# A histogram and a scatter moved between stages of a graph network kernel

## The chip, the cores and the metric

The kernel runs on one core of a Trainium2 chip. The metric is the time of one execution on the device in microseconds (us), the median of several runs. The core has five engines with an instruction stream each: PE (TensorE, matrix products), DVE (VectorE, elementwise), ACT (ScalarE), POOL (GpSimd, which here mostly issues indirect DMAs) and SP (SyncE, which issues plain DMAs and counts). They meet only in semaphores and in a barrier at the end of each block of code. `then_inc(s, n)` adds n to a semaphore when an instruction is done, a DMA adds 16 when it has landed, and `wait_ge(s, n)` holds an engine's stream.

## The reference

```
h0 = layernorm(x)                                     # x: 12500 nodes x 256
x1 = x + segment_sum(h0[src] * edge_weight, dst) @ W.T + b      # 200000 edges, dst sorted
y  = layernorm(x1)
h  = (y @ W_gat).reshape(M, 4 heads, 4 experts)
a_src, a_dst = (h * att_src).sum(-1), (h * att_dst).sum(-1)
e  = leaky_relu(a_src[src2] + a_dst[dst2], 0.2)       # 131072 unsorted edges + a loop per node
alpha = softmax of e over the edges of each destination
agg = segment_sum(h[src2] * alpha, dst2) + b_gat
scores = layernorm(agg).mean over heads;  the 2 best of 4 experts get softmax weights g
out = x1 + sum over experts of g * (gelu(y @ W1 + b1) @ W2 + b2)
```

## The kernel before

12,500 nodes are 98 tiles of 128. Six blocks of code run one after the other, with a barrier of all engines between them.

`layernorm_and_plan` normalises x into `feats` and computes which steps the next block takes. `weighted_sums` goes through the 200,000 sorted edges in 391 groups of 4x128. For each group POOL issues four indirect gathers of 128 rows of `feats` (L511) into a ring of 8 groups (`RING`); `refill(g)` waits until PE has done the last step of group g-8 (`s_mm`). SP waits for each group's gathers to land and then adds to `s_ready`, for which PE waits. For each of 488 steps (a group and a node tile) DVE builds four weighted one-hot matrices (`one_hots`, L685 and L689) at most 4 steps ahead of PE (`XS`), and PE multiplies them with the rows (L645). Where a tile ends, PE closes it and runs `stages` (L617 to L637), and ACT reads the results (`tile`), in the end h without its scale in `node_row`. Between stretches of steps DVE also sorts the 131072 second-layer edges by destination: `sort_piece(n)`, n = 0 to 23, one after each of 24 stretches, where a piece with `columns(.., 10)` is 20 TENSOR_TENSORs in a row. From piece 9 on PE turns the keys in between (L664); PE waits for the whole piece before that (`s_turn`). The whole block is 33 such stretches, of which the last 9 are one loop.

`attention_terms` scales h by 1/std, forms the attention terms of sources (`node_row`, last 4 columns) and of destinations (`node_dst`), stores both (L824), and fills `adst_first` with zeros (8 DMAs from ACT, L838).

`gather_and_experts`: POOL gathers the source's 20 values for all 131072 sorted edges, 1024 indirect DMAs (L1120), which SP moves into `states` (L1093). Meanwhile PE, ACT and DVE run the four experts of 39 of the 49 pairs of tiles (`pair`). In the first 32 pairs DVE also builds 0/1 matrices of the edges' destinations (`hots`, L1285: 16 TENSOR_TENSORs for 32 columns of edges, each with two inputs in SBUF), and PE adds up their products (`count`, L1247) to a histogram: how many edges each node has. `positions` turns it into the first and last place of each node's edges in the sorted list. After its gathers, POOL scatters the destinations' terms to those first places in `adst_first`: 98 indirect DMAs (L1139) in 14 sets of 7, each set after two small copies.

`segment_softmax` begins with the load of `adst_first` and of the last value from `adst_dram`; its scans run on DVE, with 4 pairs of experts beside them. `combine` gathers the nodes' results, weighs the experts and writes the output.

Of the kernel before, what the change touches and what calls it, by code (L numbers as in the profile page):

```python
# [5 lines left out]
F32 = mybir.dt.float32  # L6
# [32 lines left out]
HCOLS = 32  # L39
# [9 lines left out]
EARLY_PAIRS = 39  # L49
SCAN_PAIRS = 4  # L50
# [26 lines left out]
def build(nc, x, src, dst, edge_weight, W, b, W_gat, att_src, att_dst, b_gat, gamma, beta,  # L77
# [14 lines left out]
    with ExitStack() as top:  # L92
# [28 lines left out]
        with ExitStack() as part1:  # L121
# [12 lines left out]
            weighted_sums(nc, sem, feats, edge_index, x, W, b, W_gat, W1, b1, W2, b2, m)  # L134
            attention_terms(nc, sem, att_src, att_dst, m)
# [258 lines left out]
def weighted_sums(nc, sem, feats, edge_index, x, W, b, W_gat, W1, b1, W2, b2, m):  # L394
# [11 lines left out]
    with ExitStack() as ctx:  # L406
# [27 lines left out]
        squares = sb("squares", [P, FEAT])  # L434
        psA = pb("node_sums", 1024)
        psT = pb("turned", GCOLS)
        psS, psX, psY, psH = pb("sums_turned"), pb("x1_product"), pb("xc_turned"), pb("h_product")
# [10 lines left out]
        s_w, s_wt, s_wte = sem("b_weights"), sem("b_w_turned"), sem("b_w_ready")  # L448
        s_tile = sem("b_tile_summed")
# [8 lines left out]
        PIECES = 24  # L458

        CUT = [1 + (QUADS - 1) * n // (PIECES + 9) for n in range(PIECES + 1)] + [QUADS]  # L460
# [17 lines left out]

        @block.sync
        def _(sp):  # L480
# [4 lines left out]
            sp.dma_start(brow[:], b.rearrange("(a n) -> a n", a=1)).then_inc(s_w, 16)  # L485
            for k in range(HALVES):
                sp.dma_start(m.w1[:, k, :, :], W1[:, k * P:(k + 1) * P, :].rearrange("e p n -> p e n")
                             ).then_inc(s_experts, 16)
# [8 lines left out]

            with sp.Fori(1, full_rounds + 1) as i:
# [6 lines left out]
            sp.wait_ge(s_experts, 16 * (HALVES + FB + 2 * EXPERTS))  # L505

        @block.gpsimd
        def _(pool):
# [12 lines left out]
            for g in range(RING):  # L521
# [5 lines left out]
                            allow_small_or_imprecise_dtypes=True))  # L527
            pool.wait_ge(s_pc, c.n)

            for t in (sums, sums_t, xc, xc_t, xs[:, 2:XS, :]):  # L530
                c.inc(pool.memset(t[:], 0.0))
            c.inc(pool.affine_select(out=shift_dn[:], in_=shift_dn[:], compare_op=ALU.not_equal, fill=1.0,
                                     base=1, pattern=[[-1, P]], channel_multiplier=1))
            for g in range(RING, GROUPS):
                refill(g)

        @block.scalar
        def _(act):
# [47 lines left out]
            act.wait_ge(s_w, 16 * 3)  # L586
# [8 lines left out]
            with act.Fori(1, LOOPED) as u:  # L595
                for r in range(XS):
                    tile(u * XS + r, r)
            for j in range(LOOPED * XS, TILES + 4):
                tile(j, j % XS)
            for par in range(2):  # L600
# [3 lines left out]
        def _(pe):  # L604

            pe.wait_ge(s_w, 16 * 3)
# [6 lines left out]
            pe.wait_ge(s_pc, 9)  # L613
# [39 lines left out]

            open_or_close(0, True)
            for r in range(XS):
                step(r, r)
            for n in range(PIECES):
                with pe.Fori(CUT[n], CUT[n + 1]) as u:
                    for r in range(XS):
                        step(u * XS + r, r)  # L660
                if n >= 9 and n < PIECES - 1:
# [5 lines left out]

            pe.wait_ge(s_turn, PIECES - 9)
            pe.matmul(psT[:, 0:2], shift_dn[:], lastd[:], start=True, stop=True).then_inc(s_turned, 1)
            with pe.Fori(CUT[PIECES], CUT[PIECES + 1]) as u:  # L670
                for r in range(XS):
                    step(u * XS + r, r)
# [5 lines left out]
        def _(v):  # L678
# [14 lines left out]
            def sort_init():  # L693
                v.wait_ge(s_ei, 32)
                c.done(v.tensor_scalar(key_i[0], key_i[0], KEY_SHIFT, KEY_TOP, ALU.logical_shift_left,
# [3 lines left out]
                v.wait_ge(s_pc, 9)  # L699
# [87 lines left out]

            for r in range(XS):
# [3 lines left out]
            for n in range(PIECES):  # L792
# [3 lines left out]
                buf = sort_piece(n, buf)  # L796
            sort_end(buf)
            with v.Fori(CUT[PIECES], CUT[PIECES + 1]) as u:
                for r in range(XS):
                    one_hots(u * XS + r, r)  # L800

def attention_terms(nc, sem, att_src, att_dst, m):

    with ExitStack() as ctx:
        def sb(name, shape, dt=F32):
# [979 lines left out]
```

## Time and profile before

| | |
|---|---|
| runs shown (3) | 4170.54, 4172.11, 4172.34 us; median 4172.11 |
| the profiled execution | 4173.15 us, of which the profile's span is 4171.6 |
| busy in the span | PE 3043.3 us (73%), DVE 1862.1 (45%), ACT 711.1 (17%), POOL 2771.7 (66%) |
| mean PE clock | 0.859 of full speed |

A POOL instruction that issues an indirect DMA is shown as busy for some 0.95 us, with 0.30 us ahead of it that the profile calls "issue"; such a row stands for 1.25 us of POOL's time. Names in a row are the program's tiles, `out<-in`. A "q" behind an engine's name is its instruction queue. Each value of PE, both weights and data, is 32 bits wide in the steps, and the profile shows one product as two MATMUL records, so one step of four products is "x8". The ends of MATMULs are modelled, and some records can be missing.

### The profile page before, as it was taken

To read this page: it belongs to the slowest core of one execution; us is meant where nothing else is said; L and a number is where in the kernel's file an instruction comes from. 1 tells how busy PE (TensorE), PEld (TensorE's weight loads), DVE (VectorE), ACT (ScalarE), POOL (GpSimd) and SP (SyncE) were. 2 spreads that over 40 slices of the span, in tenths; PEclk is the share of its full clock that TensorE was granted. 3 is DMA by queue.
4 is the path that set the end of the run, shared out by engine and by line. 5 is a ranking of instruction groups with operands and counts; after the bars stand their busy time and mean duration, and the time that the engine had idled before them with its cause. 6 is when DMAs were issued, how large, how long until landed. Compare 5 with 4: busy or idle time off the path is not lost. (4 is left out here: it accounts for less than half of the span.)

```text
span 4171.6 us, 58590 instructions
## 1 busy us (share of the span) xinstructions
PE 3043.3 (73%) x13541; PEld 2403.4 (58%) x13542; DVE 1862.1 (45%) x4572; ACT 711.1 (17%) x1985; POOL 2771.7 (66%) x2844
## 2 busy tenths in 40 slices
PE   1356666777788887889869999999999700175946
PEld 0234444555566665666658888888888600154734
DVE  6233344535555556434434444444431000387749
ACT  4000000000111111222222222222222100031412
POOL 0677777777777777777747777777777777300850
PEclk6677878888978998999989999999999855587968
DMA  7533333344444444444422222222222210003839
GB/s 252 163 104 106 108 109 111 114 114 114 116 116 119 121 121 120 127 127 127 130 87 63 60 63 60 65 63 60 63 61 66 48 19 5 31 23 154 311 139 358
DMA packets 298251, 450.16 MB, mean 108 GB/s; under 512 B 61256, under 2 KB 232339, under 8 KB 297491
## 3 DMA queue, kind: packets, MB, share of 16 engines
q0 software_dynamic: 114144, 216.61, 21.1%
q1 hardware_dynamic: 83238, 137.78, 9.2%
q10 hardware_dynamic: 100749, 94.40, 6.9%
q8 instruction: 48, 0.79, 0.1%
q14 instruction: 72, 0.59, 0.0%
HBM read 330.48 MB, written 105.96 MB: 105 GB/s over the span
## 5 line engine op out<-in xcount | busy, mean ns | idle before, releaser
L511 POOL DMA_INDIRECT rows<-feats,src_t x1564 | 1506.1, 963 | 589.6 <-issue 464.5
L645 PE MATMUL node_sums<-rows,hot 128*128 x3904 | 1088.3, 435 | 452.2 <-SPq L501 428.2
L645 PEld LDWEIGHTS node_sums<-rows,hot 128*128 128x128 f32 x3904 | 809.2, 215 | 694.1 <-issue 567.6
L1120 POOL DMA_INDIRECT got<-row_dram,src_sorted x1024 | 994.6, 971 | 311.9 <-issue 311.9
L689 DVE TENSOR_SCALAR hot<-iota,rel,ew_t 128x128 f32<-128x128 f32 x1952 | 558.5, 363 | 64.7 <-DVE rel L685 1.8
L1210 PE MATMUL d_hidden<-d_yt,w 128*128 128x256 f32 x2496 | 569.0, 382 | 0.8 <-DVE d_yt L1310 0.8
L1221 PE MATMUL d_expert<-w,hid 128*128 128x256 f32 x2496 | 564.1, 379 | 0.0
L685 DVE TENSOR_SCALAR rel<-dst_t,step_base 128x4 f32 x488 | 126.8, 260 | 976.5 <-PE node_sums L645 924.3
L1221 PEld LDWEIGHTS d_expert<-w,hid 128*128 128x128 f32 x2496 | 475.1, 190 | 63.6
L1210 PEld LDWEIGHTS d_hidden<-d_yt,w 128*128 128x128 f32 x2496 | 471.3, 191 | 62.0 <-DVE d_yt L1310 1.2
L1295 DVE TENSOR_TENSOR yo<-d_expert,b2r 128x512 f32<-128x512 f32 x156 | 107.9, 692 | 705.2 <-PE d_expert L1221 705.2
L1164 ACT ACTIVATE hid<-d_hidden,b1c 128x256 f32<-128x256 f32 x624 | 262.0, 471 | 887.2 <-PE d_hidden L1210 887.2
L553 ACT COPY sums<-node_sums 128x256 f32<-128x256 f32 x98 | 36.5, 372 | 1691.1 <-PE sums_turned L637 1691.1
L960 PE MATMUL scan_ps_y_turned<-ident,scan_y 128*128 128x128 f32 x16 | 2.9, 313 | 310.3 <-ACT scan_y L897 310.3
L960 PEld LDWEIGHTS scan_ps_y_turned<-ident,scan_y 128*128 128x128 f32 x16 | 2.2, 160 | 311.0 <-ACT scan_y L897 310.7
L1622 POOL DMA_INDIRECT ns<-state_dram,last_pos x98 | 155.7, 1589 | 30.4 <-issue 29.6
L1285 DVE TENSOR_TENSOR hot_lo<-iota_b,lo 128x512 bf16<-128x512 bf16 x256 | 160.7, 697 | 0.0
L1618 POOL MEMSET ns<- 128x2352 f32 x1 | 2.1, 2057 | 237.3 <-POOLq L1362 237.3
L1743 DVE SCALAR_TENSOR_TENSOR xs<-ys,sc,xs 128x256 f32<-128x256 f32 x392 | 156.2, 479 | 5.5 <-DMA xs<-x_dram 4.9
L1455 DVE COPY decay<-adfirst 128x4 f32<-128x4 f32 x1 | 0.2, 165 | 307.8 <-DMA adfirst<-adst_dram,dst_first 307.8
L1285 DVE TENSOR_TENSOR hot_hi<-iota_b,hi 128x392 bf16<-128x392 bf16 x256 | 124.7, 560 | 0.0
L1139 POOL DMA_INDIRECT adst_first<-sdat,sidx x98 | 96.3, 983 | 38.1 <-issue 26.9
(292 smaller groups left out, 2831.3 us busy)
## 6 DMA issues: line engine op xcount, KB each, us to landing
ys<-y_dram SPq DMA_DIRECT2D x49, 1024.0 KB, 10.0
y_dram<-yo ACTq DMA_DIRECT2D x156, 256.0 KB, 2.3
rows<-feats,src_t POOLq DMA_INDIRECT x1564, 2.8
got<-row_dram,src_sorted POOLq DMA_INDIRECT x1024, 2.4
feats<-xout SPq DMA_DIRECT2D x14, 896.0 KB, 4.9
x_dram<-x ACTq DMA_DIRECT2D x98, 128.0 KB
xs<-x_dram SPq DMA_DIRECT2D x49, 256.0 KB, 10.9
x_ring<-in_x ACTq DMA_DIRECT2D x97, 128.0 KB
```

The source lines that it names most:

```text
L511: pool.indirect_dma_start(rows[:, g % RING, j, :], None, feats, bass.IndirectOffsetOnAxis(ap=m.src_t[:, g * GT + j:g * GT + j + 1], axis=0 ...
L645: t = pe.matmul(psA[:, ds(((code >> 1) & 1) * 512, FEAT)], hot[:, r, j, :], rows[:, ds((code >> 2) & (RING - 1), 1), j, :], start=False, s ...
L685: v.tensor_scalar(rel[:, r, :], m.dst_t[:, ds(g * GT, GT)], m.step_base[:, ds(s, 1)], None, ALU.subtract).then_inc(s_rel, 1)
L689: t = v.tensor_scalar(hot[:, r, j, :], m.iota[:], rel[:, r, j:j + 1], m.ew_t[:, ds(g * GT + j, 1)], ALU.is_equal, ALU.mult)
L1120: pool.indirect_dma_start(got[:, k, j, 0:ROWF], None, m.row_dram, bass.IndirectOffsetOnAxis(ap=m.src_sorted[:, n * GB + j:n * GB + j + 1], ...
L1164: t = act.activation(hid[:, e % 2, 2 * q + f, :], psL[(e % 2) * 2 + q][:, f, :], ACT.Gelu, bias=b1c[:, e, 2 * q + f:2 * q + f + 1])
L1210: t = pe.matmul(psL[(e % 2) * 2 + q][:, f, :], w1[:, h, e, (2 * q + f) * P:(2 * q + f + 1) * P], yt[:, k, h, :], start=(h == 0), stop=(h = ...
L1221: q = pe.matmul(psO[e % 2][:, t, :], hid[:, e % 2, f, t * P:(t + 1) * P], w2[:, f, e, :], start=(f == 0), stop=(f == FB - 1))
L1285: o = v.tensor_tensor(t[:, a:a + STRIP, :], iota_b[:, None, 0:wide].to_broadcast([P, STRIP, wide]), part[:, ds(q * HCOLS + a, STRIP)][:, : ...
L1295: v.tensor_tensor(yo[:, e, :, :], psO[e % 2][:], b2r[:, e:e + 1, :].to_broadcast([P, 2, FEAT]), ALU.add).then_inc(s_yo, 1)
L1622: pool.indirect_dma_start(ns[:, t, :], None, m.state_dram, bass.IndirectOffsetOnAxis(ap=m.last_pos[:, t:t + 1], axis=0), bounds_check=GEDG ...
L1743: q = v.scalar_tensor_tensor(xs[:, k, t, :], ys[:, k, t, e, :], sc[:, ds(i * (2 * SLOTS) + (2 * k + t), 1), e], xs[:, k, t, :], ALU.mult, ...
```

## The change

- `hots`, `count` and `positions` go from `gather_and_experts` to `weighted_sums`. Pieces of the histogram are 16 columns of edges instead of 32, 64 pieces instead of 32, with two buffers; four pieces follow the steps of each of the first 16 stretches (now called units, 33 of them), ahead of the sort piece. The matrices' number and shapes stay the same.
- `attention_terms` is no block of its own. Its work stands at the end of `weighted_sums`, for tiles 0 to 87 and then 88 to 97 (`TERMS`). The zeros for `adst_first` are stored by SP early in `weighted_sums`, ahead of SP's loop that adds to `s_ready`.
- The 98 scatters read `first_pos` and `node_dst` directly, without copies: 22 at the end of `weighted_sums`, after the first part of the terms, and 76 at the head of `gather_and_experts`, ahead of the gathers.
- `psS` and `psY` share one PSUM tile, so that the counts get one.

```diff
-HCOLS = 32
+HCOLS = 16
+TERMS = [0, 88, TILES]
+SPREAD_BEFORE = 22
...
+def spread(pool, m, t):
+    pool.indirect_dma_start(m.adst_first, bass.IndirectOffsetOnAxis(ap=m.first_pos[:, t:t + 1], axis=0),
+                            m.node_dst[:, t, :], None, bounds_check=GEDGES - 1, oob_is_err=False
+                            ).then_inc(m.s_sc, 16)
...
# weighted_sums, sync
+            sp.wait_ge(s_pc, PC)
+            for q in range(8):
+                sp.dma_start(flat[q], zeros[:]).then_inc(s_zo, 16)
             with sp.Fori(1, full_rounds + 1) as i:
...
+            for q in range(len(TERMS) - 1):
+                for n, (d, t) in enumerate(((m.row_dram, m.node_row), (m.adst_dram, m.node_dst))):
+                    sp.wait_ge(s_row, 2 * q + n + 1)
+                    sp.dma_start(d.rearrange("(p t) c -> p t c", p=P)[:, TERMS[q]:TERMS[q + 1], :],
+                                 t[:, TERMS[q]:TERMS[q + 1], :]).then_inc(s_fin, 16)
+            sp.wait_ge(s_fin, 16 * 2 * (len(TERMS) - 1))
# weighted_sums, gpsimd
             for g in range(RING, GROUPS):
                 refill(g)
+            pool.wait_ge(s_pos, 1)
+            pool.wait_ge(s_zo, 16 * 8)
+            pool.wait_ge(s_row, 2)
+            for t in range(SPREAD_BEFORE):
+                spread(pool, m, t)
# weighted_sums, tensor
+            def count(q):
+                pe.wait_ge(s_hh, q + 1)
+                for j in range(HCOLS):
+                    t = pe.matmul(psC[:, 0:TILES], hot_lo[:, q % 2, j, :], hot_hi[:, q % 2, j, :],
+                                  start=False, stop=False)
+                t.then_inc(s_hm, 1)
...
+            for n in range(UNITS):
                 with pe.Fori(CUT[n], CUT[n + 1]) as u:
                     for r in range(XS):
                         step(u * XS + r, r)
+                if n < COUNTED:
+                    for q in range(PER):
+                        count(n * PER + q)
# weighted_sums, vector
+            def hots(q):
+                if q >= 2:
+                    v.wait_ge(s_hm, q - 1)
+                for part, wide, t in ((lo, P, hot_lo), (hi, TILES, hot_hi)):
+                    for a in range(0, HCOLS, STRIP):
+                        o = v.tensor_tensor(t[:, q % 2, a:a + STRIP, :], ...
+                o.then_inc(s_hh, 1)
...
+            def terms(q):
+                a, b = TERMS[q], TERMS[q + 1]
+                v.wait_ge(s_evac, b + 5)
...
                     for r in range(XS):
                         one_hots(u * XS + r, r)
+                if n < COUNTED:
+                    for q in range(PER):
+                        hots(n * PER + q)
+                if n == COUNTED:
+                    positions()
+                if n < PIECES:
+                    buf = sort_piece(n, buf)
...
+            for q in range(len(TERMS) - 1):
+                terms(q)
# gather_and_experts, gpsimd
+            for t in range(SPREAD_BEFORE, TILES):
+                spread(pool, m, t)
...
             for n in range(BATCHES):
                 batch(n)
-            for k in range(2):
-                spread(0, k, first=True)
...
+            pool.wait_ge(m.s_sc, 16 * TILES)
# gather_and_experts, tensor and vector
-                    count(u * 2 + k)
...
-                    if count and e < 2:
-                        hots(i, e)
```

POOL's stream from the last gathers of `feats` (L511) to the first of `row_dram` (L1120), before:

```order
L511 DMA rows<-feats,src_t 128x256 x4
L406 UNCONDITIONAL_BRANCH
L827 UNCONDITIONAL_BRANCH
L829 MEMSET zeros 128x512
L804 UNCONDITIONAL_BRANCH
L1102 UNCONDITIONAL_BRANCH
L1105 IOTA iota_b 128x128
L1107 MEMSET zero_b 128x128
L1108 MEMSET before 128x128
L1109 MEMSET got 128x1536
L1112 AFFINE_SELECT before<-before 128x128
L1120 DMA got<-row_dram,src_sorted 128x20 x1024
```

and of the change (the lines have moved: L556 are the gathers of `feats`, L1179 those of `row_dram`):

```order
L556 DMA rows<-feats,src_t 128x256 x4
L397 DMA adst_first<-node_dst,first_pos 131072x4 x22
L414 UNCONDITIONAL_BRANCH
L1167 UNCONDITIONAL_BRANCH
L1169 MEMSET got 128x1536
L397 DMA adst_first<-node_dst,first_pos 131072x4 x76
L1179 DMA got<-row_dram,src_sorted 128x20 x1024
L1125 UNCONDITIONAL_BRANCH
```

The scatters stood behind the 1024 gathers, and now stand ahead of them, 22 in the block before.

PE's stream in the change, from the end of the first unit's steps to the next unit's; before, the loop's branch was followed directly by the next loop:

```order
L716 UNCONDITIONAL_BRANCH
L734 REGISTER_ALU
L734 COMPARE_AND_BRANCH
L725 MATMUL counts<-hot_hi,hot_lo 128x98 [waits b_hist_hot]
L725 MATMUL counts<-hot_hi,hot_lo 128x98 x15
L725 MATMUL counts<-hot_hi,hot_lo 128x98 [waits b_hist_hot]
L725 MATMUL counts<-hot_hi,hot_lo 128x98 x15
L725 MATMUL counts<-hot_hi,hot_lo 128x98 [waits b_hist_hot]
L725 MATMUL counts<-hot_hi,hot_lo 128x98 x15
L725 MATMUL counts<-hot_hi,hot_lo 128x98 [waits b_hist_hot]
L725 MATMUL counts<-hot_hi,hot_lo 128x98 x15
```

PE now waits four times for DVE's matrices between two units, with all later steps behind it.

SP's stream in the change, from the loads of weights to the loop that adds to `s_ready` (L536):

```order
L524 DMA w<-in_L_ffn_W 128x4x256 x4
L527 DMA b2r<-in_L_ffn_b 128x256 x4
L530 DMA b1c<-in_L_ffn_b 128x4x1 x4
L535 DMA adst_first<-zeros 128x512 x8
L536 UNCONDITIONAL_BRANCH
```

The eight stores of zeros, which ACT issued in `attention_terms`, now stand ahead of the loop that PE's first step waits for.

## Rows read from the trace of the kernel before

**Rows 1.** Windows: start:end and length, busy time (instructions) by engine, clock.

```profile
2400.00:2800.00 400.00, 400.00 (x2207) 353.90 (x2206) 174.66 (x311) 90.80 (x217) 305.24 (x312) 1.00 0.27 62
...
3400.00:3500.00 100.00, 0.00 (x0) 0.00 (x0) 0.00 (x0) 0.00 (x0) 74.16 (x86) 0.50 0.10 13
```

**Rows 2.** Who waited for whom: total us, times, longest.

```profile
POOL rows L511 <- issue: 464.5, 1525, 0.3
...
POOL rows L511 <- PE node_sums L645: 17.5, 38, 6.2
```

**Rows 3.** Timeline around the end of weighted_sums: start, us, instruction.

```profile
2100.77 1.12 DVE L689 TENSOR_SCALAR hot<-iota,rel,ew_t 128x128 f32<-128x128 f32 x4
...
2104.01 0.95 POOL L511 DMA_INDIRECT rows<-feats,src_t  x1 [0.30 <-issue]
...
2136.53 0.54 DVE L844 TENSOR_SCALAR mean<-mean 128x98 f32<-128x98 f32 x1 [34.65 <-PEq L406]
...
2147.18 0.33 SPq L824 DMA_DIRECT2D adst_dram<-node_dst  x1
...
2149.79 0.24 POOL L1105 IOTA iota_b<- 128x128 bf16 x1 [12.78 <-POOLq L804]
...
2150.26 1.37 POOL L1109 MEMSET got<- 128x1536 f32 x1
...
2152.17 0.96 POOL L1120 DMA_INDIRECT got<-row_dram,src_sorted  x1 [0.16 <-issue]
```

**Rows 4.** Timeline where gather_and_experts ends.

```profile
3458.52 0.20 POOL L1134 COPY sidx<-first_pos 128x7 int32<-128x7 int32 x1
...
3596.71 0.98 POOL L1139 DMA_INDIRECT adst_first<-sdat,sidx  x1 [0.30 <-issue]
3607.39 0.32 SPq L1395 DMA_DIRECT2D decay<-adst_first  x1
```

**Rows 5.** POOL's drains: duration min/median/max ns, first and last start.

```profile
L406 POOLq DRAIN  x1: 20718/20718/20718, 2089.9 to 2089.9; - x1
...
L1040 POOLq DRAIN  x1: 8067/8067/8067, 3599.1 to 3599.1; - x1
```

**Rows 6.** Windows of the gathers alone: of row_dram (L1120), then of feats (L511).

```profile
2173.00:3102.00 929.00, 708.99 (x723) 1.00 0.27 62
3110.00:3310.00 200.00, 151.24 (x161) 1.00 0.28 63
...
700.00:1500.00 800.00, 608.39 (x630) 0.84 0.41 116
1720.00:2100.00 380.00, 287.95 (x303) 0.97 0.44 127
```

**Rows 7.** Groups: line, engine, op, shapes xcount | busy us, mean ns | idle before.

```profile
L1285 DVE TENSOR_TENSOR hot_lo<-iota_b,lo 128x512 bf16<-128x512 bf16 x256 | 160.7, 697 | 0.0
...
L1285 DVE TENSOR_TENSOR hot_hi<-iota_b,hi 128x392 bf16<-128x392 bf16 x256 | 124.7, 560 | 0.0
...
L1247 PE MATMUL counts<-hot_hi,hot_lo 128*128 128x98 bf16 x1024 | 51.5, 207 | 0.0
```

**Rows 8.** Timeline: PE's and POOL's start in weighted_sums; the stores of zeros.

```profile
158.74 15.50 PE L645 MATMUL node_sums<-rows,hot 128*128 x56 [1.08 <-issue]
...
163.35 0.97 POOL L511 DMA_INDIRECT rows<-feats,src_t  x1 [6.20 <-PE node_sums L645]
...
2137.04 4.98 ACTq L838 DMA_DIRECT2D adst_first<-zeros  x8
```

**Rows 9.** Timeline: a close, steps at high and at low clock; a sort block.

```profile
1170.79 0.28 PE L617 MATMUL node_sums<-b_zeros 1*128 1x256 bf16 x1
...
1174.35 3.72 PE L645 MATMUL node_sums<-rows,hot 128*128 x16
...
1205.23 3.15 PE L645 MATMUL node_sums<-rows,hot 128*128 x8 [2.24 <-SPq L501]
...
1314.49 0.69 DVE L730 TENSOR_TENSOR src_sorted<-seg_keep 128x512 f32<-128x512 f32 x1
```

More of the change, by code:

```diff
@@ L477, in weighted_sums @@
                     cur = 1 if cur == 2 else 1 - cur
+        PC = 13
         @block.sync
@@ L527, in _ @@
                             allow_small_or_imprecise_dtypes=True))
+            c.inc(pool.iota(iota_b[:], pattern=[[1, P]], base=0, channel_multiplier=0,
+                            allow_small_or_imprecise_dtypes=True))
+            c.inc(pool.memset(before[:], 1.0))
+            c.inc(pool.memset(zeros[:], 0.0))
             pool.wait_ge(s_pc, c.n)
@@ L652, in step @@
                     open_or_close((d + 1) & 1, True)
+            def count(q):
[4 more added lines that the diff above has]
+                t.then_inc(s_hm, 1)
             open_or_close(0, True)
+            pe.matmul(psC[:, 0:TILES], zero_b[:, 0:P], zero_b[:, 0:TILES], start=True, stop=False)
             for r in range(XS):
                 step(r, r)
-            for n in range(PIECES):
+            for n in range(UNITS):
                 with pe.Fori(CUT[n], CUT[n + 1]) as u:
@@ L666, in _ @@
                     t.then_inc(s_turned, 1)
[L668 to L672, printed above, removed]
+                if n == PIECES - 1:
+                    pe.wait_ge(s_turn, PIECES - 9)
+                    pe.matmul(psT[:, 0:2], shift_dn[:], lastd[:], start=True, stop=True).then_inc(s_turned, 1)
             open_or_close(TILES & 1, False)
@@ L791, in _ @@
             buf = 2
-            for n in range(PIECES):
+            for n in range(UNITS):
                 with v.Fori(CUT[n], CUT[n + 1]) as u:
@@ L1242, in pair @@
                         layer2(i * EXPERTS - 1, EXPERTS - 1)
[L1244 to L1248 removed]
             turn(0)
             pair(0, 0, first=True)
[L1252 to L1261 removed]
+            with pe.Fori(0, (EARLY_PAIRS - 1) // 2 - 1) as u:
                 for k in range(2):
@@ L1310, in out_of_psum, with pair @@
                 v.tensor_copy(yt[:, k, :, :], psY[:]).then_inc(s_yt, 1)
-            def pair(i, k, first=False, between=None, count=False):
+            def pair(i, k, first=False):
                 more = not (isinstance(i, int) and i == EARLY_PAIRS - 1)
@@ L1316, in pair @@
                 for e in range(EXPERTS):
-                    if e == 3 and between:
-                        between()
                     outs(i * EXPERTS + e, e, i, first=first)
```

260 lines of the change are left out of this document (97 added, 163 removed).

## The prediction, made before the changed kernel ran

> **What bounds the kernel now.** I read the windows first, then the waits, then the timeline around each barrier. In the middle of `gather_and_experts` PE is busy all the time and POOL issues 312 gathers in 400 us; but by 3400 PE, DVE and ACT stand still with all their pairs done, and only POOL works [rows 1], up to the block's end at 3607 [rows 4]. In `weighted_sums` POOL's idle time is nearly all its own issue, 464.5 us in 1525 pieces of 0.3, and only 17.5 us are a wait for PE, of which one of 6.2 is real [rows 2]. So POOL's stream sets the end of both blocks: 1564 gathers, a gap of 48.2 us from the last one to the first of the next block [rows 3], 1024 gathers, 98 scatters [rows 4]. What the change takes from PE or DVE in `gather_and_experts` is worth nothing by itself. What counts is what it does to POOL.
>
> **The change part by part.** The sum is made against the profiled execution's own 4173.15 us.
>
> Scatters. Before, they take from 3458.52 to 3597.69, 139.2 us for 98; one is 0.98 us and 0.30 of issue, 1.28, the rest are the copies ahead of each set and the wait for them [rows 4]. 76 without copies take 97.3. **-41.9 us.**
>
> The 22 others. DVE's last one-hot ends at 2101.9. The terms took from 2136.53 to about 2147.1 for 98 tiles [rows 3]; for 88, mostly in proportion, 9.6 us, so they are there at 2111.5, and POOL, free since 2105.0, waits for them. 22 x 1.28 = 28.2, and some 0.3 for the wait, put its last scatter's end at 2140.0. Then comes the drain. After the 98 scatters it ended at 3607.2, 9.5 us behind the last instruction; after the `feats` gathers at 2110.6, 5.6 behind [rows 5]. I take the scatters' figure: drained at 2149.5, POOL's first instruction of the next block at about 2150.1, against 2149.79 before [rows 3]. By the two ends this is +0.3 or -3.6; I take **+0.3**. PE's and ACT's tail ended by 2136.5 [rows 3], the ten last tiles' terms and their stores (under 2 + 2 us) hide under the scatters: without that cover the block would end at 2141. In the next block one MEMSET of 1.37 us stands ahead of the first indirect DMA, where 2.4 us of constants and zeros stood [rows 3]: **-1.0**.
>
> The tail. Behind the last scatter 9.7 us pass until the next block's first load [rows 4]. Now gathers are last, and the drain behind gathers took 5.6 [rows 5]; SP's last move should be shorter than that. **-3.8** (bounds 0 and -4).
>
> DVE's matrices. While they run, POOL issues 723 gathers in 929 us, 1.285 each; behind them, with the experts still on PE and DVE, 161 in 200, 1.242 [rows 6], and a single one shows 0.30 + 0.95 or 0.96, 1.25 [rows 3]. Over the 723 this is 25 us by the 1.25 and 31 by the 1.242; I take 28, for 285.4 us of DVE time [rows 7]. They have two inputs in SBUF. The same shape of slowing shows in `weighted_sums` beside the sort's TENSOR_TENSORs: 1.270 against 1.254 [rows 6]. So the tax moves along with the matrices: **-28** in one block, **+28** in the other. The bounds for the second are 12 (the sort's difference of 0.016 on the 758 gathers of 16 of 33 units) and 31; I take 28, since it is the same instruction. The Trainium skill (SBUF — State Buffer, "Who interferes with whom") has the rule: a DVE instruction with two SBUF inputs contends with a GpSimd instruction that reads SBUF, and the later one blocks fully. If POOL were shut out for all of DVE's 285 us the tax would be 285 and not 28; rows 6 decide, and the sum by the rule is the same, since it is taken and given back.
>
> SP's zeros. PE's first step needs `s_ready`, and SP now issues 8 stores ahead of the add. ACT took 4.98 us for the same eight. PE began at 158.74 and POOL went on at 163.35, behind PE's first group [rows 8]. Both come later by the stores: PE at 163.7. Nothing covers it: POOL's ring is full. **+5.0** (bounds 3, if some of the stores lie beside the work that PE waits for anyway, and 9, if SP is nearly twice as slow at it as ACT).
>
> The matrices' place in a unit. A unit is 14.7 steps and three closes, and POOL needs 1564 x 1.27 / 33 = 60.2 us for it [rows 6], 62 with the tax. PE needs 1.86 us a step, 3.56 for a close [rows 9]: 38 us, and 0.8 for each of four counts [rows 7], in later units some 2.5 for the transposes: 44. But PE now stops in every unit. DVE is at most 4 steps ahead, two buffers let it build two pieces under that lead, and the other two, 4.5 us each [rows 7], run while PE waits. Behind them stands the sort piece, in units 9, 11, 13 and 15 20 TENSOR_TENSORs of 0.69 [rows 9] and (but for 9) a copy, 15 us, and the first new pair of one-hots, some 1.75, of which 1.12 are the second's [rows 3]. That is a stop of 26 us, and 70 us for the unit against 62. The units between have sort pieces of 3 to 7 us and come to 58 to 61. What stands ahead of POOL is the ring: 8 groups x 5.1 = 41 us, less the group in issue and the one landing, some 31. So one stop is just covered, and a backlog on top of it isn't. I take 5 us of POOL's wait for each of the last three long units: **+15** (bounds 0, all covered, and 40, ten for each of four). DVE's conversions and `positions` (some 3 and 5 us) are in the same cover.
>
> Sum: -41.9 + 0.3 - 1.0 - 3.8 - 28 + 28 + 5.0 + 15 = -26.4; 4173.15 - 26.4 = 4146.7. The runs' median, 4172.11, lies 1.0 below the profiled run: **4146**.
>
> **The rivals.** *No change* (within 0.2%, 4164 to 4180): the waits in the long units take 33 to 49 us instead of 15. For it speaks that the stop is within a few us of the ring's depth; against it that sort blocks of 14 us [rows 9] cost POOL nothing now [rows 2]. Time at 40: 4171.
>
> *Slower, PE becomes the bound of units 5 to 15.* A step at low clock took 3.15 us beside 1.86 [rows 9], a close then some 6.0. If each stop of 20 to 26 us sends PE to the low level for its next three steps and one close, a unit is 6 to 7 us longer: the four long ones are 15 over POOL's pace, the three between 3, units 6 to 8 about 7, in sum 90, less the ring's 31 once: 59 us of waits, 4190. It decides from 34 us more than I take, that is 49 us of waits. Against it: PE's very start, behind the block's constants, held POOL for no more than 6.2 us [rows 8], and there is slack again after unit 15. The Trainium skill (TensorE: Matmul & The Clock Gate, "HAM oscillation") says that the clock falls to half in such gaps each time, and that every burst behind one starts slow: by that rule this rival is the expected one, at 4190, and my +15 is too small. In this trace the steps behind waits are of both lengths, 1.86 and 3.15 us within 31 us of each other [rows 9], so I weigh it lightly.
>
> *The tax stays behind.* If the matrices fall where POOL waits anyway, or cost the `feats` gathers less, the 28 us are gained and not given back: 4118 at the least, and with the sort's price 4130.
>
> *The terms come late.* If the first terms are ready only with PE's tail, at 2146, POOL's scatters end 34 us later: 4181. DVE waits for tile 92's results, and they are there 100 us before: unlikely.
>
> **How the numbers follow.** About 0.2% (8 us) is what a measurement of this kernel can tell from no change. The forecast, 4127 to 4163, has 0.68, the tax left behind, from 4118, has 0.09, no change 0.14, slower 0.09 (0.07 the low clock, 0.02 the terms). The range leaves out little below and the slower cases above: 4126 to 4175. Faster 0.77, same 0.14, slower 0.09.
>
> **What would show it.** POOL's cadence in the first 16 units near 1.305 (1.270 and 0.036), and 1.25 in all of `gather_and_experts`; the first POOL wait for PE near 11 us (6.2 and 5.0); more such waits only near units 11, 13 and 15; the last `feats` gather at 2104 + 5 + 28 + 15 = 2152; 22 scatters beginning 8 us behind it; the next block 45 us behind it; `gather_and_experts` from there in 1383 us instead of 1458. It would be wrong if POOL's waits for PE come in most of the 16 units or are over 33 us, if SP's stores take twice as long, or if the drain behind the 22 scatters is longer than 10 us.

## The result, and the profile after

The changed kernel takes 4234.8 us (median of 4 runs, 4205 to 4248) where the kernel before takes 4172.2 (4170.5 to 4173.1): a ratio of 1.014, with an interval of 1.0119 to 1.0161. The forecast was 4146, in a range from 4126 to 4175, so the sign was wrong. The profiled execution took 4229.80 us, and 4173.15 before. The runs also spread over 43 us, where those before lay within 3.

The costliest groups of the profile after (line, engine, operation, tiles, count | busy us, mean ns | idle before):

```profile
L556 POOL DMA_INDIRECT rows<-feats,src_t x1564 | 1632.9, 1044 | 597.8 <-issue 464.0 <-POOLq L147 108.0 <-PE node_sums L713 25.7
...
L1179 POOL DMA_INDIRECT got<-row_dram,src_sorted x1024 | 967.4, 945 | 311.9 <-issue 311.9
```

The same groups of the kernel before, and its third group of gathers, in `combine`:

```profile
L511 POOL DMA_INDIRECT rows<-feats,src_t x1564 | 1506.1, 963 | 589.6 <-issue 464.5 <-POOLq L146 107.6 <-PE node_sums L645 17.5
...
L1120 POOL DMA_INDIRECT got<-row_dram,src_sorted x1024 | 994.6, 971 | 311.9 <-issue 311.9
...
L1622 POOL DMA_INDIRECT ns<-state_dram,last_pos x98 | 155.7, 1589 | 30.4 <-issue 29.6 <-POOL ns L1618 0.8
```

Busy time in the 1564 gathers of `feats` was 1506.1 us before and is 1632.9 now, 126.8 more. The 1024 gathers of `row_dram` went the other way, from 994.6 to 967.4, which is the 28 us that the forecast took out of that block (27.2). Where the 126.8 lie is seen in the spread of single instructions (duration in ns, min/median/max, first and last start):

```profile
L556 POOL DMA_INDIRECT rows<-feats,src_t x1564: 942/947/9642, 114.9 to 2239.7; - x196
...
L1179 POOL DMA_INDIRECT got<-row_dram,src_sorted x1024: 940/945/1067, 2382.1 to 3660.2; - x171
```

The median is as before, 947 ns, but one gather lasted 9642 ns. In the timeline there are 13 that last between 8.5 and 9.6 us, one in each of 13 of the 16 units with matrices. Together they are 103.8 us over normal ones. Nearly all of the remaining 23 us is in gathers of 1.05 to 1.5 us beside matrices (21.9 us over normal ones). This is the first unit, DVE's and POOL's rows (some of POOL's between are left out):

```profile
193.48 1.11 DVE L772 TENSOR_SCALAR hot<-iota,rel,ew_t 128x128 f32<-128x128 f32 x4
...
194.51 2.49 DVE L881 TENSOR_TENSOR hot_lo<-iota_b,lo 128x512 bf16<-128x512 bf16 x4
195.21 8.83 POOL L556 DMA_INDIRECT rows<-feats,src_t  x1 [0.30 <-issue]
...
196.92 1.99 DVE L881 TENSOR_TENSOR hot_hi<-iota_b,hi 128x392 bf16<-128x392 bf16 x4
198.82 2.49 DVE L881 TENSOR_TENSOR hot_lo<-iota_b,lo 128x512 bf16<-128x512 bf16 x4
201.23 1.99 DVE L881 TENSOR_TENSOR hot_hi<-iota_b,hi 128x392 bf16<-128x392 bf16 x4
...
223.15 2.53 DVE L881 TENSOR_TENSOR hot_lo<-iota_b,lo 128x512 bf16<-128x512 bf16 x4 [19.93 <-PE counts L725]
...
225.60 2.03 DVE L881 TENSOR_TENSOR hot_hi<-iota_b,hi 128x392 bf16<-128x392 bf16 x4
...
226.86 1.12 POOL L556 DMA_INDIRECT rows<-feats,src_t  x1 [0.30 <-issue]
227.56 2.48 DVE L881 TENSOR_TENSOR hot_lo<-iota_b,lo 128x512 bf16<-128x512 bf16 x4
...
228.28 1.37 POOL L556 DMA_INDIRECT rows<-feats,src_t  x1 [0.31 <-issue]
```

The one-hots (TENSOR_SCALAR, L772) go over into the first two pieces of matrices (16 TENSOR_TENSORs, L881) without a pause. The gather that POOL begins at 195.21 ends at 204.04, 0.82 us behind the end of the run at 203.22: it was held from the start. The second pair of pieces, which DVE begins after a wait for PE, is the same 16 instructions, and beside it gathers take 1.12 and 1.37 at the worst. So it is in all units: behind the one-hots a gather is held in 13 of 16, behind the wait in none of 16. Each hold costs some 8 us, so different numbers of them would account for the spread of the runs; that was not counted run by run.

POOL's waits for PE grew by 8 us, from 17.5 to 25.7, and the start is close to the forecast (who waited for whom: total us, times, longest; then the timeline of the start):

```profile
POOL rows L556 <- issue: 464.0, 1522, 0.6
...
POOL rows L556 <- PE node_sums L713: 25.7, 41, 9.5
```

```profile
159.14 4.45 SPq L535 DMA_DIRECT2D adst_first<-zeros  x8
...
164.31 8.70 PE L713 MATMUL node_sums<-rows,hot 128*128 x32 [4.60 <-SPq L539]
...
168.62 0.97 POOL L556 DMA_INDIRECT rows<-feats,src_t  x1 [9.50 <-PE node_sums L713]
```

PE begins 5.6 us later than in [rows 8] and POOL's first wait is 9.5 us instead of 6.2. The other waits over 0.5 us are three, 4.9 us together.

The rest of the program did what the sum said. First POOL's drain at the end of `weighted_sums`:

```profile
L414 POOLq DRAIN  x1: 22866/22866/22866, 2260.4 to 2260.4; - x1
```

The timeline at the edges of the two blocks:

```profile
2247.85 1.01 POOL L397 DMA_INDIRECT adst_first<-node_dst,first_pos  x1 [6.88 <-DVEq L921]
...
2283.51 1.38 POOL L1169 MEMSET got<- 128x1536 f32 x1 [7.67 <-POOLq L414]
...
3660.18 0.94 POOL L1179 DMA_INDIRECT got<-row_dram,src_sorted  x1 [0.30 <-issue]
...
3666.66 0.33 SPq L1366 DMA_DIRECT2D decay<-adst_first  x1
```

The window of the gathers of `row_dram` alone, with DVE's matrices gone:

```profile
2400.00:3300.00 900.00, 680.67 (x721) 1.00 0.28 65
```

Scatters begin 8.2 us behind the start of the last gather of `feats` (2247.85 less 2239.7), `gather_and_experts` runs from 2283.5 to 3666.7, which is 1383.2 us, and its gathers come every 1.248 us from the start (900 / 721), close to the 1.242 of the second window of [rows 6].

### The profile page after: what moved, and what is told of

Read it like the earlier page. It is cut to its first block and busy times, and to the rows that moved or that the text cites. A ratio compares the mean times of both kernels' runs of the same rounds, so it can differ in the third digit from the quotient of the medians.

```text
span 4228.1 us, 58027 instructions
## 1 busy us (share of the span) xinstructions
PE 3003.1 (71%) x13541; PEld 2395.4 (57%) x13542; DVE 1856.1 (44%) x4580; ACT 711.4 (17%) x1986; POOL 2866.2 (68%) x2815
## 5 line engine op out<-in xcount | busy, mean ns | idle before, releaser
L556 POOL DMA_INDIRECT rows<-feats,src_t x1564 | 1632.9, 1044 | 597.8 <-issue 464.0
L713 PE MATMUL node_sums<-rows,hot 128*128 x3904 | 1035.7, 421 | 392.9 <-SPq L539 268.6
L1179 POOL DMA_INDIRECT got<-row_dram,src_sorted x1024 | 967.4, 945 | 311.9 <-issue 311.9
L713 PEld LDWEIGHTS node_sums<-rows,hot 128*128 128x128 f32 x3904 | 790.4, 209 | 603.1 <-issue 479.5
L772 DVE TENSOR_SCALAR hot<-iota,rel,ew_t 128x128 f32<-128x128 f32 x1952 | 557.6, 362 | 64.3 <-DVE rel L768 0.3
L881 DVE TENSOR_TENSOR hot_lo<-iota_b,lo 128x512 bf16<-128x512 bf16 x256 | 160.3, 685 | 204.5 <-PE counts L725 204.5
L725 PE MATMUL counts<-hot_hi,hot_lo 128*128 128x98 bf16 x1024 | 71.5, 241 | 110.1 <-DVE hot_hi L881 110.1
L725 PEld LDWEIGHTS counts<-hot_hi,hot_lo 128*128 128x128 bf16 x1024 | 64.1, 117 | 118.5 <-DVE hot_hi L881 115.5
L881 DVE TENSOR_TENSOR hot_hi<-iota_b,hi 128x392 bf16<-128x392 bf16 x256 | 127.6, 556 | 0.0
```

The lines of the kernel that those rows point to most:

```text
L556: pool.indirect_dma_start(rows[:, g % RING, j, :], None, feats, bass.IndirectOffsetOnAxis(ap=m.src_t[:, g * GT + j:g * GT + j + 1], axis=0 ...
L713: t = pe.matmul(psA[:, ds(((code >> 1) & 1) * 512, FEAT)], hot[:, r, j, :], rows[:, ds((code >> 2) & (RING - 1), 1), j, :], start=False, s ...
L725: t = pe.matmul(psC[:, 0:TILES], hot_lo[:, q % 2, j, :], hot_hi[:, q % 2, j, :], start=False, stop=False)
L772: t = v.tensor_scalar(hot[:, r, j, :], m.iota[:], rel[:, r, j:j + 1], m.ew_t[:, ds(g * GT + j, 1)], ALU.is_equal, ALU.mult)
L881: o = v.tensor_tensor(t[:, q % 2, a:a + STRIP, :], iota_b[:, None, 0:wide].to_broadcast([P, STRIP, wide]), part[:, q * HCOLS + a:q * HCOLS ...
L1179: pool.indirect_dma_start(got[:, k, j, 0:ROWF], None, m.row_dram, bass.IndirectOffsetOnAxis(ap=m.src_sorted[:, n * GB + j:n * GB + j + 1], ...
```

## The experiments

"Held" stands for a gather that lasts till 0.8 to 1.2 us behind the end of a run of DVE instructions, instead of its usual 0.95 us. The theories: **A**, DVE's run of two-input instructions holds POOL's gather as long as the run lasts, if DVE comes into it in a certain way; **B**, any run of 16 can do so, when a gather meets it at the wrong moment; **C**, PE's stops between the units cost the time. Two of the chips (runs e1 to e4, and h0, h1, f1, g1) took 5840 to 5850 us for the kernel before; PE issued late beside POOL's gathers there, and POOL's instructions no longer set the end. From them single rows are used; times count from the others.

### A wait ahead of the run

```diff
             def hots(q):
+                if q % PER == 0:
+                    v.wait_ge(s_hot, CUT[q // PER + 1] * XS)
```

> The changed kernel, with one wait of DVE for its own last one-hot of the unit ahead of the first new matrix of each unit; all work is kept. In the trace of the change, 13 gathers of POOL last 8.5 to 9.6 us, 103.8 us over a normal one, and each ends with a run of 16 back-to-back TENSOR_TENSORs that follows the one-hots (TENSOR_SCALAR) without a pause; the 16 runs that DVE begins after a wait for PE block nothing. Theory A (what DVE did directly ahead decides: the run takes over the port from the one-hots and POOL never gets in): no gather over 2 us, some 2 us of the small tax come back for each of the 13, so 4230 - 104 + 22 = 4148 us (4140 to 4156), and runs within 0.3% of each other. Theory B (the run of 16 itself blocks when a gather meets it at a certain moment; the pause of under 0.1 us changes nothing but the moment): about the same number of long gathers, 8 to 16, 4190 to 4250. Theory C (PE's waits in the units cost the time): no change from 4235.

Measured: 6096 us against 5849. Of the 16 runs behind the one-hots one held a gather, for 5.1 us, which came out of a wait of its own in the middle of the run. B expected 8 to 16. The time says nothing here, and was taken again beside the change:

> The changed kernel itself, as the measure for the three beside it. Its earlier runs went from 4205 to 4248 us. Theory A (each long gather costs some 8 us, and how many there are differs from run to run): again 10 to 16 long gathers in its trace, each behind the one-hots of a unit, none in the pairs that follow a wait for PE, 4200 to 4250 us. Theory C (waits for PE): the spread has to show as different waits of POOL for PE.

> The changed kernel with DVE's wait for its own last one-hot ahead of the first matrix of each unit, again, beside the change itself on a chip on which before takes its usual time (else the ratio to the change counts). Theory A: at most 1 long gather, 4148 us (4140 to 4156), 0.979 of the change, and a narrow spread. Theory C: as the change.

Measured on another chip of that kind: the change 6025 us with 14 gathers over 4 us, the one with the wait 6095 us with one. Fewer holds, and no shorter: POOL's waits for PE grew from 446.6 to 644.6 us. On a chip where the kernel before takes 4174.6:

> The changed kernel with DVE's wait ahead of each unit's matrices, once more, for its time on a chip on which the kernel before takes 4172 us: on the two chips of the runs so far before took 5840 us, PE issued its instructions late beside POOL's gathers, and a sum of POOL's instructions did not set the time. Theory A: no or one long gather, 4140 to 4156 us. Theory B or C: over 4190.

Measured: 4155.2 us (5 runs, 4152 to 4157), a ratio to the kernel before of 0.995 (0.9937 to 0.9964). The spread is 5 us. The gathers' durations:

```profile
L556 POOL DMA_INDIRECT rows<-feats,src_t x1564: 942/949/1474, 115.2 to 2164.5; - x196
```

POOL's waits for PE, and DVE's timeline in the first unit:

```profile
POOL rows L556 <- PE node_sums L713: 43.0, 52, 12.0
```

```profile
193.94 1.11 DVE L772 TENSOR_SCALAR hot<-iota,rel,ew_t 128x128 f32<-128x128 f32 x4
195.09 2.58 DVE L883 TENSOR_TENSOR hot_lo<-iota_b,lo 128x512 bf16<-128x512 bf16 x4
```

The longest gather is 1474 ns. The moment at which a gather meets the run does not explain this: three of these runs had a gather begin 0.22 us behind their start and let it through in 1.29 us, while in the change one that began at 0.24 us was held for 9.30 us. That speaks against B. A pause of 0.04 us between the one-hots and the matrices (193.94 + 1.11 to 195.09) is all that this kernel adds, and by the two ratios it is 1.9% or 80 us faster than the change.

### An instruction ahead of the run instead of a wait

```diff
+                if q % PER == 0:
+                    v.tensor_reduce(spare_out[:, q // PER:q // PER + 1], m.iota[:], AX_X, ALU.add)
```

> The changed kernel, with one TENSOR_REDUCE over 128x128 ahead of the first new matrix of each unit and no wait; its result is used nowhere. Theory A in the form that a pause is needed: the long gathers stay, 4205 to 4250. Theory A in the form that the kind of the instruction ahead decides (the one-hots hold the port, a reduction lets it go): no gather over 2 us, 4148 + 16 x 0.2 of DVE's time that is hidden: 4140 to 4156. Theory B: 8 to 16 long gathers, as before.

Measured: 6034 us; 16 gathers held in 16 units, 152 us over normal ones. Where DVE made four pieces at a stretch, a hold was 17.4 us or more (min/median/max):

```profile
L557 POOL DMA_INDIRECT rows<-feats,src_t x1564: 940/946/18278, 113.4 to 2826.6; - x196
```

So a reduction between does not let the gather in; the pause does (one held in 16 on the same chip), and the hold is as long as the run.

### A wait between two pieces

```diff
+                if q % 2 == 1:
+                    v.wait_ge(s_hh, q)
```

> The changed kernel, with one wait of DVE for its own last instruction between two pieces of matrices that follow each other, and none ahead of the first; all work is kept. Theory A: a gather that meets the first piece is held till the end of that piece and no longer, so long gathers of some 4.2 us instead of 8.8, 13 of 16: 4230 - 13 x 4.4 + 13 x 0.8 = 4183 us (4170 to 4195). Theory B: the block needs the length of 16, so none is left: 4148; or the same number of blocks in either piece: up to 32 places, 4180 to 4240.

Measured: 6051 us, on a chip where before takes 5849; 14 gathers of 3.3 to 5.0 us, 50 us over normal ones, each released at the end of the first piece. And with its time:

> The changed kernel with DVE's wait for its own last instruction between two pieces and none ahead of the first, for its time on a chip on which before takes 4172 us. On another chip it held 13 gathers by 3.7 us each, always to the end of the first piece. Theory A: 10 to 16 gathers of 4 to 5 us, 4157 + 13 x 3.3 = 4200 us less what of these delays hides POOL's waits for PE: 4175 to 4205, between the change and the kernel with the wait ahead (4155).

```profile
L556 POOL DMA_INDIRECT rows<-feats,src_t x1564: 940/946/5323, 115.3 to 2187.4; - x196
```

```profile
POOL rows L556 <- PE node_sums L713: 34.7, 54, 9.8
```

Measured: 4181.4 us (7 runs, 4177 to 4187), 12 gathers of 4.3 to 5.3 us, 44.5 us over normal ones (the rows above: durations, and waits for PE). Half the run, half the hold, and the time lies between the change (4235) and the kernel with no hold (4155), as A expected.

### What stands ahead of the run

One TENSOR_SCALAR of the one-hots' form ahead of the runs of matrices in `gather_and_experts`, in the kernel before:

```diff
             def hots(q, n):
+                v.tensor_scalar(ahead_out[:, n, :], m.iota[:], m.ones[:, 0:1], m.ones[:, 1:2],
+                                ALU.is_equal, ALU.mult)
```

> The kernel before, with one TENSOR_SCALAR of the one-hots' form (128x128, float32, two scalars per partition) directly ahead of each of the 64 runs of 8 matrices in gather_and_experts; its result is used nowhere. There a run follows a TENSOR_TENSOR or a COPY that reads PSUM, and in 64 runs no gather lasts over 1.3 us. Theory A by kind: most runs now hold one gather to their end, 64 x (some 4 us less 0.5) x 0.8 = 180 us on POOL's stream: 4300 to 4400 us. Theory A by pause, or a block that only the gathers of feats or the place in weighted_sums can have: under 4182 (64 x 0.3 us of DVE's time are hidden, a little more tax).

Measured: 5850 us against 5849, and no gather over 2.1 us. That spoke against the kind. But the trace shows only six of these runs with a gather beside them. Two sharper forms followed: three TENSOR_SCALARs, ahead of the runs of `hot_lo` alone, again in the kernel before; and four of them in the change, ahead of the second pair of pieces, behind its wait.

```diff
+                for j in range(3 * (n == 0)):
+                    v.tensor_scalar(ahead_out[:, j, :], m.iota[:], m.ones[:, 0:1], m.ones[:, 1:2],
+                                    ALU.is_equal, ALU.mult)
```

> The kernel before with three TENSOR_SCALARs of the one-hots' form ahead of each of the 32 runs of hot_lo in gather_and_experts; their result is used nowhere. One of them ahead of a run held nothing in the runs that the trace showed on another chip. Theory A by kind alone: 32 x 0.8 x 4 us = 100 us more, 4270 (4230 to 4310). If these gathers (80 bytes a row) or runs of 8 are safe: no gather over 2 us, 4172 to 4185.

Measured: 4291.9 us (4 runs, 4290 to 4296), 120 us slower than the kernel before. Its gathers' durations, and one run of `hot_lo` in the timeline, DVE's rows and then POOL's:

```profile
L1121 POOL DMA_INDIRECT got<-row_dram,src_sorted x1024: 940/944/5380, 2151.6 to 3577.4; - x171
```

```profile
2201.43 0.69 DVE L1299 TENSOR_TENSOR yo<-d_expert,b2r 128x512 f32<-128x512 f32 x1 [5.53 <-PE d_expert L1222]
2202.04 0.85 DVE L1286 TENSOR_SCALAR ahead_out<-iota,ones 128x128 f32<-128x128 f32 x3
2202.80 4.90 DVE L1289 TENSOR_TENSOR hot_lo<-iota_b,lo 128x512 bf16<-128x512 bf16 x8
```

```profile
2202.33 0.94 POOL L1121 DMA_INDIRECT got<-row_dram,src_sorted  x1 [0.30 <-issue]
2203.58 4.94 POOL L1121 DMA_INDIRECT got<-row_dram,src_sorted  x1 [0.30 <-issue]
```

All 32 runs of `hot_lo` held one gather each to their end, 128 us over normal ones, while the runs of `hot_hi`, which follow a COPY from PSUM as before, held none. Before this edit the same 32 runs, behind a TENSOR_TENSOR that reads PSUM, held none. The edit also moved the gather's start from some 0.3 to some 0.8 us behind the run's; that this alone does it is unlikely, since in the change a gather at 0.79 us, beside a run behind a wait, took 1.32 us.

```diff
                 if q >= 2:
                     v.wait_ge(s_hm, q - 1)
+                if q % PER == 2:
+                    for j in range(GT):
+                        v.tensor_scalar(ahead_out[:, j, :], m.iota[:], m.ones[:, 0:1], m.ones[:, 1:2],
+                                        ALU.is_equal, ALU.mult)
```

> The changed kernel with four TENSOR_SCALARs of the one-hots' form ahead of the second pair of pieces in each unit, behind its wait for PE; their result is used nowhere. In the change the first pair, behind the one-hots, held a gather in 13 of 16 units, and the second, behind a wait, in none. Theory A by kind (TENSOR_SCALARs with one SBUF input ahead of the run begin the block): long gathers in the second pairs too, 12 to 16 more, 4235 + 13 x 8 = 4340 us (4310 to 4370). Theory A by place (what counts is that the one-hots' last result is waited for, or where the unit's loop ends): the second pairs stay free, 4205 to 4255.

The group of its gathers of `feats`:

```profile
L557 POOL DMA_INDIRECT rows<-feats,src_t x1564 | 1749.8, 1119 | 595.9 <-issue 462.7 <-POOLq L147 108.4 <-PE node_sums L714 24.7
```

Measured: 4323.0 us (5 runs, 4313 to 4348); 29 gathers held in 32 places, 239 us over normal ones: 15 of the 16 first pairs and 14 of the second, which were safe in the change. Some of them began 0.30 us behind the start of the run, where gathers in the kernel before, beside `hot_lo` behind an instruction that reads PSUM, lasted 1.2 us.

### The histogram back in its old block

The matrices, counts and `positions` in `gather_and_experts` as before, and all 98 scatters, without copies, behind the gathers.

> The changed kernel with the histogram (matrices, counts, positions) back in gather_and_experts, and therefore all 98 scatters behind the gathers, without copies; terms in two parts and SP's zeros as in the change. All work is kept. Theory A, whose whole loss lies in the matrices' place: no long gather; weighted_sums ends its gathers at 2105 + 3.8 = 2109; the tail of the terms ends it near 2142, so -7 at the block's edge; scatters without copies -13.8; sum -21, 4151 us. If the terms, the zeros or the missing copies cost something of their own: over 4165.

Measured: 5888 us against 5840, a ratio of 1.0091, on a chip of the other kind. No gather was held. But POOL waited 900 us for `positions` there, so the time tells nothing about the expected 21 us; it was not run elsewhere, and that the other parts of the change cost nothing of their own is not shown by this run.

### Matrices from one input

`lo` and `hi` also become float32 here, since they are now read as scalars.

```diff
-                    for a in range(0, HCOLS, STRIP):
-                        o = v.tensor_tensor(t[:, q % 2, a:a + STRIP, :], ...
+                    for a in range(HCOLS):
+                        o = v.tensor_scalar(t[:, q % 2, a, :], iota_b[:, 0:wide],
+                                            part[:, q * HCOLS + a:q * HCOLS + a + 1], None, ALU.is_equal)
```

> The changed kernel with the matrices made column by column with TENSOR_SCALAR (one input of 128 or 98 values, and a column of edges as scalars) instead of TENSOR_TENSOR with two inputs: 32 instructions for a piece instead of 8. All work is kept. If the second input in SBUF is what holds POOL out: no long gather, and no gathers of 1.1 to 1.4 us beside the matrices. A piece takes 32 x (0.15 to 0.36) = 5 to 11.5 us instead of 4.5, so PE stops longer: at 5 us 4120 to 4150, at 11.5 us PE becomes the bound of 16 units, some 20 us more in each, 4400. If any run of back-to-back DVE instructions that follows the one-hots holds POOL out, whatever its inputs: 13 to 16 gathers as long as two pieces.

Measured: 6190 us on the same chip, no gather held. On a chip where the kernel before takes 4174.6:

> The changed kernel with the matrices made column by column from one input, for its time on such a chip. A column takes 0.18 us, a piece of 32 instructions 5.6 us instead of 4.5. Theory A (two inputs in SBUF hold POOL): no long gather and no small tax, so 4230 - 104 - 28 = 4098 us plus some 2.3 us for the longer stop in each of the four long units, and what of the tax hid waits: 4105 to 4135. If PE becomes the bound of units by the longer stops: over 4150.

Its groups of gathers and matrices:

```profile
L556 POOL DMA_INDIRECT rows<-feats,src_t x1564 | 1510.7, 966 | 629.3 <-issue 462.5 <-POOLq L147 107.3 <-PE node_sums L713 59.5
...
L881 DVE TENSOR_SCALAR hot_lo<-iota_b,lo 128x128 bf16<-128x128 bf16 x1024 | 176.5, 285 | 66.8 <-PE counts L725 66.8
L881 DVE TENSOR_SCALAR hot_hi<-iota_b,hi 128x98 bf16<-128x98 bf16 x1024 | 167.1, 276 | 0.0
```

Measured: 4141.0 us (5 runs, 4137 to 4146), a ratio of 0.9918 (0.9905 to 0.9932), which is above the expected 4105 to 4135. No gather beside the matrices was held; the longest of all, 2.39 us, stands beside a TENSOR_TENSOR of 1.62 us in the terms. Busy time in the gathers is 1510.7, within 5 us of the 1506.1 before the matrices came into this block, against 1543.6 with two inputs and the wait ahead. What keeps it from the 4105 is PE: POOL waits 59.5 us for it, 9.8 of them at the start and 8.4, 1.8, 7.1 and 19.6 in the four long units.

### The best version

One input; three pieces in each of the first 8 units and two in the next 20; SP's zeros in the middle of its loop.

```diff
-        COUNTED = 16
-        PER = HPIECES // COUNTED
+        COUNTS = [3] * 8 + [2] * 20
...
+            landed(1, 36)
             sp.wait_ge(s_pc, PC)
             flat = m.adst_first.rearrange("(q p n) c -> q p (n c)", q=8, p=P)
             for q in range(8):
                 sp.dma_start(flat[q], zeros[:]).then_inc(s_zo, 16)
+            landed(36, full_rounds + 1)
```

> The changed kernel with one-input matrices (TENSOR_SCALAR, column by column), three pieces in each of the first 8 units and two in each of the next 20 instead of four in 16, positions behind unit 27, and SP's eight stores of zeros in the middle of its loop (behind round 35) instead of ahead of it. All work is kept. i2_one_input had 59.4 us of POOL's waits for PE: 9.8 at the start and 8.4, 1.8, 7.1 and 19.6 in the four long units. Theory A: the start goes back to 6.2 (-3.6), the long units' stops are shorter by two pieces and two counts (13 us), which ends their waits (-36 or nearly): 4141 - 36 = 4105 us (4100 to 4118). If stops in the later units, where PE transposes keys and POOL has the same pace, add up instead: 4125 to 4160.

POOL's waits for PE:

```profile
POOL rows L562 <- PE node_sums L719: 40.2, 58, 11.2
```

Measured: 4112.6 us (4 runs, 4110 to 4117) against 4171.8, a ratio of 0.9855 (0.9839 to 0.9872), with all work kept. The first wait is back at 6.2 us, and the four long units wait no more. Later ones do, 3.9, 11.2 and 2.4 us between 1570 and 1710. This is 59 us faster than the kernel before and 122 faster than the change.

## Why the prediction was wrong

**The step that failed** is the one on DVE's matrices, its bound above all: "The bounds for the second are 12 [...] and 31; I take 28, since it is the same instruction." In the new place the matrices cost POOL 126.8 us, 103.8 of them in 13 held gathers. The instruction is indeed the same. What differs is what DVE did directly ahead of it: an instruction that reads PSUM in the old place, TENSOR_SCALARs from SBUF to SBUF in the new one, with no pause. The bounds were taken from two rows in which nothing was held, and the text then said that the hold would change nothing, "since it is taken and given back". That is true only if both places hold alike, and the runs j3 and j4 show that they do not: three or four TENSOR_SCALARs ahead turn a harmless run into one that holds, in either block.

**The rows that should have set the upper bound** were in the trace of before, in `combine`, and the prediction did not read them. DVE there runs 80 SCALAR_TENSOR_TENSORs with two inputs in SBUF at a stretch; POOL's timeline first, then DVE's:

```profile
3899.16 1.24 POOL L1622 DMA_INDIRECT ns<-state_dram,last_pos  x1 [0.30 <-issue]
3900.70 1.28 POOL L1622 DMA_INDIRECT ns<-state_dram,last_pos  x1 [0.30 <-issue]
3902.29 29.14 POOL L1622 DMA_INDIRECT ns<-state_dram,last_pos  x1 [0.30 <-issue]
3931.74 1.00 POOL L1622 DMA_INDIRECT ns<-state_dram,last_pos  x1 [0.30 <-issue]
...
3952.15 29.00 POOL L1622 DMA_INDIRECT ns<-state_dram,last_pos  x1 [0.30 <-issue]
```

```profile
3898.27 0.24 DVE L1734 TENSOR_TENSOR sc<-f_ge,one 128x80 f32<-128x80 f32 x1
3898.65 31.76 DVE L1743 SCALAR_TENSOR_TENSOR xs<-ys,sc,xs 128x256 f32<-128x256 f32 x80
```

One gather of 29.14 us, till 1.0 us behind the end of the run (3898.65 + 31.76 = 3930.41), and one of 29.00 us beside the next run of 80: both runs that POOL's gathers meet there hold one. The mean of that group beside the two others shows it at once: 1589 ns a gather in `combine`, 963 and 971 in the others. Carried over, the upper bound for the new place is DVE's time in the matrices, 285 us, and a rival on the slow side belonged beside it: half the pieces held, 140 us. The Trainium skill (SBUF — State Buffer, "Who interferes with whom") says that the later of two such instructions fully blocks until the other one is done. The traces agree that a gather can be shut out, for 29.14 us here and 8.83 above, but not on how long: these are the lengths of 80 and 16 instructions, which take 0.5 to 0.7 us each. Nor is a gather always shut out, since beside the 16 runs behind a wait none took over 1.42 us. Against the rule the prediction set an average, 0.10 us for each us of DVE, which was true of runs that hold nothing.

**The other terms.** -41.9, -1.0 and the -28 in `gather_and_experts`: with the -3.8 for the block's end they gave 1383 us, and it took 1383.2. The edge between the blocks: 45.1 us from the end of the last gather of `feats` to the first instruction of the next block was the forecast, with the drain over 9.5 us behind the last scatter; it was 42.5, with the drain over after 7.5 (2260.4 + 22.9 = 2283.3). SP's zeros: +5.0 forecast, 4.45 us for the stores, and 3.3 in POOL's wait. The long units: +15 forecast. In the change itself it was 4.9. In i1, without holds, it was 18.8 (5.3, 0.8, 0.8 and 12.0), which fits that a POOL that is held gives PE time. The small slowing, +28 forecast, was 37.5 in i1 (1543.6 less 1506.1). So without the holds the sum comes out at 4146 + 9.5 + 3.8 - 1.7 - 2.6 = 4155, and i1 took 4155.2. That the two agree to the microsecond is luck: two of the terms are the change's and not i1's, and on i1's chip the kernel before took 2.4 us more.

**The rivals.** "Slower, PE becomes the bound" gave 4190 and the right sign with the wrong cause: POOL's waits for PE are 25.7 us, and C is out. (Against this rival the prediction read 1.86 and 3.15 us as steps behind waits. The one of 1.86 stands behind none; behind a wait of 1.92 us a step took 1.99, so the reading of both lengths holds.) "The tax stays behind" does not come by itself, but by a change of the instruction: i2 has it.

**What stays open.** Which property of a run lets it hold. Shown are: 13 of 16 and 29 of 32 runs behind three or four TENSOR_SCALARs in `weighted_sums`, and 32 of 32 in `gather_and_experts`, hold; behind a pause of 0.04 us, or behind an instruction that reads PSUM, nearly none does. But a hold needs no TENSOR_SCALARs ahead: in `combine` a TENSOR_TENSOR and a pause of 0.14 us stand there, two gathers get in, and the third is held, and in e1 a gather was held that began 4.4 us into a run behind a wait. One TENSOR_SCALAR held nothing in the six places where its trace shows it. The moment has a part too, which no run tested by itself. Behind TENSOR_SCALARs a gather that began 0.01 to 0.02 us behind the run's start got through in all nine places where the traces of the change, h0, e3, j3 and j5 show one (two of the change's three free units are such; the third met one at 0.27 us, where others at 0.24 and 0.30 us were held). Those that began 0.03 us ahead of it, or 0.12 us behind, were held.

## What to carry to other kernels

Before vector work moves beside a GpSimd engine that issues DMAs, look at the longest instruction in GpSimd's groups as well as at the mean: two gathers of 29 us in another block showed here what such a run can cost. A run of vector instructions with two inputs in SBUF can cost GpSimd its whole length, and what stands ahead of the run can decide whether it does. A wait of the vector engine for its own last result, which left a pause of 0.04 us ahead of the run, took the holds away; one-input instructions took the small slowing away too, at a fifth more vector time (344 us instead of 288).

## What the runs showed of the hardware

- The same 16 TENSOR_TENSORs with the same operands made one gather 7.6 to 8.7 us longer in the change, or each gather 0.0 to 0.5 us, and in most cases what stood ahead decided which. A held gather ends 0.8 to 1.2 us behind the end of the run, whether this is 4.4, 8.7, 17.3 or 31.8 us long.
- A TENSOR_REDUCE between the TENSOR_SCALARs and the run did not help (16 of 16 held); a wait did.
- TENSOR_SCALARs of 128 or 98 bfloat16 values with a float32 scalar per partition, 2048 of them in i2, back to back in groups of up to 64, took 0.17 us each (343.6 / 2048) and slowed the gathers by less than 5 us in sum.
- Two chips (that of e1 to e4, and that of f1, g1, h0 and h1) ran the kernel before in 5840 to 5850 us instead of 4172. Beside POOL's gathers PE issued one MATMUL every 2.8 us there, at the lower clock (0.50 of full speed from 3400 to 3600), with nothing that it waited for in the profile. POOL issued 142 gathers in these 200 us, against 161 in 200 us of the change on a usual chip. With POOL idle, from 4300 to 4700 in e4, PE was busy all the time at full clock. Why these chips differ is not known. Timelines of PE and of POOL in the change on such a chip (h0):

```profile
3502.86 0.58 PE L1255 MATMUL d_expert<-w,hid 128*128 128x256 f32 x1 [2.21 <-issue]
3505.66 0.58 PE L1255 MATMUL d_expert<-w,hid 128*128 128x256 f32 x1 [2.22 <-issue]
```

```profile
3500.75 0.94 POOL L1179 DMA_INDIRECT got<-row_dram,src_sorted  x1 [0.30 <-issue]
```
